# The column numbers of the one-hot compare, moved from SBUF to a PSUM bank in layer 1

## What is computed

```
x   = layernorm(x + L0(x, src, dst, w))
h1  = x @ lin1_w.T
c   = 0.5 * (cos(w * pi / 10) + 1)
f   = softplus(edge_attr @ nn_w1.T + nn_b1) - log 2
W   = (softplus(f @ nn_w2.T + nn_b2) - log 2) * c[:, None]
msg = W * h1[dst]                            # one row of 128 floats for each edge
agg = segment_sum(msg, src, num_segments=n)  # summed by SOURCE node
x   = layernorm(x + (h1 + agg) @ lin2_w.T + lin2_b)
```

## Time and profile before

| | |
|---|---|
| runs | 9219.49, 9211.46, 9218.32 us; median 9218.32 |
| the profiled execution | 9222.2 us, its span 9220.4 us |
| layer 0, edges | 160 to 4430 us |
| layer 1, tiles alone | 4630 to 5678 us |
| layer 1, tiles beside sums | 5678 to 8829 us |
| tail | 8835 to 9116 us |
| last stage | 9116 to 9220 us |

### The profile page before, as it was taken

The page is one execution under the profiler, slowest core; times in us unless marked ns, Lnnn a source line. Parts: engine busy times, 40 slices in busy tenths (PEclk is TensorE's granted clock), DMA queues, the critical chain, the costliest instruction groups (busy, mean ns, idle before and its releaser), DMA issues. The chain is left out here.

```text
span 9220.4 us, 203371 instructions
## 1 busy us (share of the span) xinstructions
PE 5956.5 (65%) x34966; PEld 4786.6 (52%) x35238; DVE 6490.4 (70%) x20440; ACT 3473.7 (38%) x6781; POOL 6304.8 (68%) x6541
## 2 busy tenths in 40 slices
PE   1666666666666666666655555666666666666687
PEld 1444444444444444444444445666666666666676
DVE  7777777777777776666655555777777777777776
ACT  2333333333333333333544443333333333333302
POOL 2777777777677767777167777777777777777720
PEclk8666676677667767777855556888888888888897
DMA  3444444444444444444444445666666666666676
GB/s 99 146 146 145 143 143 144 143 148 147 139 142 146 145 141 145 146 148 143 145 135 133 135 135 162 207 206 207 207 207 209 206 206 205 205 209 204 206 231 208
DMA packets 805241, 1537.36 MB, mean 167 GB/s; under 512 B 193150, under 2 KB 206900, under 8 KB 804707
## 3 DMA queue, kind: packets, MB, share of 16 engines
q1 hardware_dynamic: 595415, 1097.64, 37.4%
q0 software_dynamic: 209456, 436.16, 16.0%
q10 hardware_dynamic: 348, 3.33, 0.1%
HBM read 971.97 MB, written 564.58 MB: 167 GB/s over the span
## 5 line engine op out<-in xcount | busy, mean ns | idle before, releaser
L1229 POOL DMA_INDIRECT sorted_messages<-rows,sidx x3224 | 3216.1, 998 | 1153.9 <-issue 933.9
L433 POOL DMA_INDIRECT xg<-x_rows,gidx x3224 | 3046.9, 945 | 1362.7 <-issue 1028.7
L476 PE MATMUL bank<-onehot,xg 128*128 128x42 f32 x6448 | 1120.5, 326 | 1419.3 <-DMA xg<-x_rows,gidx 1406.7
L476 PEld LDWEIGHTS bank<-onehot,xg 128*128 128x128 f32 x6448 | 1004.2, 232 | 1496.8 <-DMA xg<-x_rows,gidx 1481.5
L482 PE MATMUL bank<-attr,nn 128*128 128x512 f32 x1612 | 1467.8, 1066 | 3.9 <-DVE hid L507 2.4
L1157 PE MATMUL bank<-hot,block_rows 128*128 128x128 f32 x8256 | 1392.3, 345 | 33.8 <-DVE hot L1311 32.2
L1157 PEld LDWEIGHTS bank<-hot,block_rows 128*128 128x128 f32 x8256 | 1348.2, 258 | 54.3 <-issue 30.1
L1127 PE MATMUL bank<-w_nn2T,e_hid 128*128 128x128 f32 x6448 | 1040.7, 314 | 289.6 <-DMA e_hid<-hidden 281.7
L1127 PEld LDWEIGHTS bank<-w_nn2T,e_hid 128*128 128x128 f32 x6448 | 1009.3, 226 | 245.6 <-DMA e_hid<-hidden 212.3
L1138 PE MATMUL bank<-h1w,ohT 128*128 128x128 bf16 x3224 | 355.9, 278 | 1072.0 <-DVE ohT L1258 1072.0
L1282 DVE SCALAR_TENSOR_TENSOR rows<-filt,meta,bank 128x128 f32<-128x128 f32 x3224 | 904.7, 343 | 94.7 <-DVE filt L1273 55.1
(11 more groups left out here) (183 smaller groups left out, 7716.5 us busy)
## 6 DMA issues: line engine op xcount, KB each, us to landing
block_rows<-sorted_messages SPq DMA_DIRECT2D x346, 792.0 KB
hidden<-hid SPq DMA_DIRECT2D x404, 512.0 KB
e_hid<-hidden SPq DMA_DIRECT2D x403, 512.0 KB
sorted_messages<-zero SPq DMA_DIRECT2D x403, 264.0 KB
dstb<-dst SPq DMA_DIRECT2D x403, 256.0 KB
attr<-attr_cols SPq DMA_DIRECT2D x403, 204.0 KB
xg<-x_rows,gidx POOLq DMA_INDIRECT x3224, 5.1
sorted_messages<-rows,sidx POOLq DMA_INDIRECT x3224
```

The costliest lines, as they stand in the source:

```text
L433: pool.indirect_dma_start(xg[s][:, :], None, x_rows, bass.IndirectOffsetOnAxis(ap=gidx[s // HALF][:, s % HALF:s % HALF + 1], axis=0),).the ...
L476: nc.tensor.matmul(bank[0][:, 0:WIN], xg[s][:, :], onehot[:, s, :], start=(s == 0), stop=(s == SUB - 1)).then_inc(summed, 1)
L1229: pool.indirect_dma_start(table, bass.IndirectOffsetOnAxis(ap=sidx[b][h][:, s:s + 1], axis=0), rows[b][h][:, s, :], None).then_inc(landed[ ...
```

## The change

DVE copies `cols` once, at the start of layer 1's edges, into the first 128 columns of bank 7, and the one-hot of a block takes its column numbers from there. The block's places and the result stay in SBUF. A wait for the copy stands ahead of the first one-hot. Nothing else differs; the tail has its four block buffers as before.

```
+    node_cols = bank[7][:, 0:P]
...
-    hot_set, summed1, added = (sem(n) for n in ("hot_set", "summed1", "added"))
+    hot_set, summed1, added, cols_set = (sem(n) for n in ("hot_set", "summed1", "added", "node_cols_set"))
...
-                dve.tensor_tensor(hot[u][:, :, :], cols[:, :].rearrange("p (o n) -> p o n", o=1).broadcast_to([P, HALF, P]),
+                dve.tensor_tensor(hot[u][:, :, :], node_cols.rearrange("p (o n) -> p o n", o=1).broadcast_to([P, HALF, P]),
                                   block_rows[k][:, u, :, D:D + 1].broadcast_to([P, HALF, P]), ALU.is_equal).then_inc(hot_set, 1)
...
+            dve.tensor_copy(node_cols, cols[:, :]).then_inc(cols_set, 1)
             dve.memset(h1w[:, :], 0.0).then_inc(zeros_set, 1)
...
             in_pairs(dve, 0, alone, windows_of)
+            dve.wait_ge(cols_set, 1)
             for u in range(TURN):
                 hot_block(0, 0, u, 16)
```

## The result

The changed kernel takes 9093.84 us (median of 4 runs, 9093.56 to 9101.43), the kernel before 9218.90 (4 runs). The ratio is 0.9865, with a 95% interval of 0.9848 to 0.9882: 1.35% faster, 125 us. The forecast was 9108 us, range 9092 to 9146.

What follows compares the result with a forecast made beforehand. POOL's scatter issue was taken as the bound beside sums. From 9222.2 us, -111 (scatters freed) + 1 (one-hots) + 0.3 (copy) gave 9112, and 9108 us as median, the runs' median being 3.9 lower; range 9092 to 9146.

Steps and rivals of the forecast that it cites:

- What bounds the kernel: Tiles beside sums: POOL's scatter issue binds at 10.51 us a tile, and POOL waits for nobody.
- The relief: Scatters no longer held by one-hots: 0.0464 us each, times 2397, 111 us less; at most about 125 us.
- The inference from layer 0: L553 and L585, with one PSUM input, leave gathers untouched, so POOL should run untouched beside the changed one-hot.
- The one-hot's own time: DVE's one-hot, now 0.68 us, grows by nothing to 8 ns with a PSUM input; +1 us taken in total.
- What is late next: Beside sums, DVE could run at 9.84 us a tile against POOL's 10.14, so DVE doesn't become the bound.
- the margin: DVE stays 0.30 us under POOL in a tile beside sums; a one-hot growing over 0.10 us would use it up.
- rival 3: DVE becomes the bound if PSUM makes a one-hot 0.1 to 0.2 us longer: 9110 to 9200 us, chance 0.05.
- Rival 1: Nothing is freed: the one-hot's output or other input, still in SBUF, holds POOL; 9218 to 9222 us, chance 0.06.
- Rival 2: ohT takes the one-hot's place in delaying scatters beside sums: 39 us less gain, 9147 us, chance 0.06.
- my bad case: ohT meets a scatter's start in every tile: up to 0.26 us, mean perhaps 0.13 over 300 tiles.
- rival 4: Slower: the repeated PSUM read runs at half rate, +0.53 us for a one-hot; 9595 us, chance 0.03.
- The total: Whole kernel: 9108 us, 1.2% less; 9092 to 9146 was to hold 8 in 10.

Runs made afterwards that it cites:

- run 9: The changed kernel with three extra one-hot-sized DVE operations behind each of 105 tiles alone, one input in PSUM, output in SBUF: 9096.87 us.
- run 8: The changed kernel with three extra one-hot-sized DVE operations behind each of 105 tiles alone, both inputs and output in SBUF: 9110.62 us.
- Run 6: The changed kernel with one extra one-hot-sized DVE operation (PSUM and SBUF in, SBUF out) in each tile beside sums: 9106.14 us, ratio 0.9873.
- run 5: The changed kernel with three extra one-hot-sized DVE operations behind each of 105 tiles alone, both inputs in SBUF, output in PSUM: 9110.08 us.
- run 11: The changed kernel with three extra DVE operations behind each tile alone, inputs in SBUF, each writing its own tile so no wait separates them: 9137.20 us.
- run 12: The changed kernel with three extra DVE operations behind each tile alone, no wait between them, one input in PSUM: 9109.00 us, ratio 0.9882.
- run 7: The changed kernel without POOL's semaphore increment between two scatters of a half: 9093.97 us, ratio 0.9868.

## Why the prediction was right

**What bounds the kernel.** Right. None of POOL's waits beside sums was longer than 0.3 us, before or after, and the time fell by what its instructions fell.

**The relief.** Right in mechanism and, at 117 us for the 111 forecast, nearly in size. The pattern that I took (the tiles alone, 963 ns) is what the tiles beside sums came to (964). Split at the 841st scatter, with both profiles of each kernel, 114 us of the 117 lie behind it (a scatter's mean fell by 47.8 ns, from 1010.6 to 962.8, where I had 46.4) and 3 us in the tiles alone, which I had kept as they were. One trace could not show that: the first profile has 388 long scatters where its repetition has 408, and its stage is 7 us shorter. The inference from layer 0 (one input in PSUM, output in SBUF, and gathers of 945 ns beside it) carried over to scatters.

The Trainium skill's two sentences (SBUF — State Buffer, Who interferes with whom) come out unequal. That a Vector instruction with two SBUF inputs contends with a GpSimd instruction that reads SBUF agrees with the seven rows of the table above: the input's place decides, the output's doesn't. That `tensor_tensor` doesn't stall descriptor generation does not hold here: 388 to 408 scatters wait for it in the kernel before. Which of the things that POOL does for an indirect DMA needs the read, the row numbers or something else, no run here shows.

**The one-hot's own time.** Right: 683 ns by median before and after (mean 685 and 684). The extra cost of a PSUM source by the Trainium skill's table (VectorE: DVE Perf Modes, the TRN2 errata), 65 ns by the estimate, isn't there: the extra operations of run 9 took 688 ns with a PSUM input, those of run 8 took 692 without.

**What is late next.** The conclusion held (DVE doesn't bind), the margin was wrong. I had subtracted only the wait for landed scatters and called the rest DVE's own. Run 6 put 0.68 us more into each tile and the tile stayed where it was. The step that failed is "DVE could run at 9.84 us for a tile": the 1.1 us ahead of the first L1322 are a latency that other work covers, so the spare is at least the 0.58 us by which DVE got busier in run 6 (172 us over 296 tiles), and not 0.30. This made rival 3 look nearer than it was. The sign that I gave for it was missed as well: the wait for landed scatters fell from 0.67 to 0.50 us for a tile, not to about 0.3. A third of the 0.36 us by which the tile got shorter came from ohT itself, which took 0.62 us in the mean beside sums before (median 0.69) and takes 0.50 now (median 0.49). It was long where POOL had just been let go by a one-hot: then DVE waited for POOL. I had counted that as DVE's own work.

**The rivals.** Rival 1 is refuted by the result, its part on what the operation writes by runs 5 and 9. Rival 2, ohT, was at work and small: beside sums the profile before has no long scatter under ohT, the profile after 58, which is most of the 73 (the sign that I had given for this rival), but only 12 us in all over the 957 ns floor, 0.04 us for a tile against 0.13 in my bad case. That it can be as large as I feared is shown by run 11, where DVE's phase put ohT onto a scatter in 80 of some 94 tiles, 0.15 us for a tile (run 12: 70, 0.08 us). Rivals 3 and 4 did not come up.

**The total.** The median lies 14 us under the forecast and 2 us inside its range. Of the 14, 6 are the larger relief and some 8 the earlier start of the scatters, of which the prediction says nothing; by layer 0's spread, 4412.9 to 4430.5 us for its last gather over all fourteen profiles, it could as well have gone the other way. That the range held is in this part luck.

## What to carry to other kernels

When one engine issues the same instruction thousands of times, compare its mean between stages before looking at waits: 963 against 1010 ns was the whole case, and no wait named it. A DVE operation with two SBUF inputs delays a GpSimd indirect DMA that starts under it until it ends, or until a row of such operations without a break ends, and moving one input to a free PSUM bank removes that, here at no cost to the operation; it pays where GpSimd's issue is the bound. And before calling an engine nearly full, ask of each of its idle stretches whether more work would lengthen it or hide in it.

## What I had not expected of the hardware

- A wait shows up as a longer instruction on POOL, not as idle time: 0.96 us became up to 1.6 in the first profile and up to 2.7 in run 11. Nearly every long one ends 0.82 to 0.84 us after the DVE operation's end, or after the last of a row without a break.
- It goes both ways. Where POOL had come first, DVE's instruction got longer: ohT took 0.69 us instead of 0.49 in most tiles beside sums of the kernel before, an extra operation 0.74 instead of 0.68 (run 11, the third at 5203.13).
- A one-input DVE operation from int16 to bf16, 1024 elements in 0.49 us, holds POOL up in the same way (8578.54 above), while float operations of one SBUF tensor input beside it don't: of the scatters from 5678 us on that begin under L1273 or L1282 in the kernel before, none took over 0.975 us.
- Two engines that wait for each other fall into a fixed phase. DVE's extra operations began 0.02 us after a scatter's start in tile after tile (5202.04 and 5202.06 above), and what a collision costs then depends on that phase: 0.12 us for a tile with two and with three such operations, not the 0.3 to 0.8 of a random one.
- POOL's 0.305 us between indirect DMAs is there with and without a semaphore increment between them (run 7).
